# A routed two-layer network on one core: first quad of each pass taken through by itself, z moved between engines, dummy products added

## The reference, cut to what matters

```python
x = x + gnn(layernorm(x), adj, ...)   # matmul by e_weight, adjacency, then h = tanh(agg @ Wx + h @ Wh + b) over 128 steps
x = x + ffn(layernorm(x), ...)        # 16 experts, the best 2 of each token

# ffn, for its input z = layernorm(x):
topk_vals, topk_idx = top_k(z @ gate_w + gate_b, 2); topk_w = softmax(topk_vals)
h = relu(z @ w1[e] + b1[e]);  expert_out = h @ w2[e] + b2[e]
y = z + sum over the two experts of topk_w * expert_out
ffn = (y - mean(y)) / sqrt(var(y) + 1e-5) * gamma + beta
```

## Time and profile before

| | us |
|---|---|
| median of 3 runs (654.96 to 655.76) | 655.46 |
| the profiled execution | 655.11 |
| its span, first to last instruction | 653.4 |

### The profile page before, as it was taken

How to read it: one execution, slowest core, us unless ns; L and a number is a source line. 1 busy time by engine, 2 the same in 40 slices (tenths; PEclk the granted TensorE clock), 3 DMA queues, 4 the chain that set the end, 5 groups by cost and what they waited for, 6 DMA issues and landing times. The chain is left out here.

```text
span 653.4 us, 17215 instructions
## 1 busy us (share of the span) xinstructions
PE 535.4 (82%) x4144; PEld 476.4 (73%) x4144; DVE 507.6 (78%) x2512; ACT 411.0 (63%) x1343; POOL 451.3 (69%) x521
## 2 busy tenths in 40 slices
PE   1676799999889861799999999943899999999990
PEld 0566567776666650599999999941799999988890
DVE  4899269999999997488888888620499899898861
ACT  1898765555555533366666666710589889899860
POOL 8766307777777777277777777776177777777775
PEclk9988899889999965899999999975799999999995
DMA  8999913665355214479886665442997666764110
GB/s 208 254 285 271 287 50 102 213 200 170 118 168 114 88 54 124 111 241 346 264 257 198 208 199 188 153 157 72 338 332 246 216 200 204 220 187 140 48 54 15
DMA packets 112893, 119.26 MB, mean 183 GB/s; under 512 B 18346, under 2 KB 97406, under 8 KB 112801
## 3 DMA queue, kind: packets, MB, share of 16 engines
q1 hardware_dynamic: 93056, 73.55, 40.6%
q0 software_dynamic: 17152, 43.03, 18.1%
q10 hardware_dynamic: 2592, 1.64, 0.8%
HBM read 66.51 MB, written 53.77 MB: 184 GB/s over the span
## 5 line engine op out<-in xcount | busy, mean ns | idle before, releaser
L311 POOL DMA_INDIRECT out_dram<-R x136 | 135.0, 993 | 59.4 <-issue 52.2
L311 POOL DMA_INDIRECT rows_by_second<-R x136 | 136.2, 1001 | 54.2 <-issue 33.2
L311 POOL DMA_INDIRECT rows_by_first<-st x128 | 125.9, 984 | 64.4 <-issue 35.6
L1143 PE MATMUL bank<-xT,wr 128*128 128x128 f32 (+1 forms) x1152 | 155.6, 280 | 8.9 <-ACT xT L1218 8.9
L1163 PE MATMUL bank<-W,hs 128*128 x1024 | 156.9, 290 | 0.0
L1143 PEld LDWEIGHTS bank<-xT,wr 128*128 128x128 f32 x1152 | 140.8, 194 | 16.0 <-ACT xT L1218 16.0
L1243 ACT ACTIVATE hs<-bank,wr 128x128 f32<-128x128 f32 x380 | 111.8, 366 | 64.4 <-PE bank L1143 59.3
L1163 PEld LDWEIGHTS bank<-W,hs 128*128 128x128 f32 x1024 | 135.1, 192 | 3.1
L1228 ACT COPY wr<-W1b 128x258 f32 x288 | 103.5, 424 | 0.0
L1328 DVE SCALAR_TENSOR_TENSOR R<-bank,R 128x128 f32<-128x128 f32 x272 | 82.2, 344 | 24.5 <-PE bank L1163 24.5
L670 ACT ACTIVATE HT<-bank,bcol 128x128 f32<-128x128 f32 x128 | 47.0, 367 | 66.6 <-PE bank L573 65.6
(11 more groups left out here) (171 smaller groups left out, 896.2 us busy)
## 6 DMA issues: line engine op xcount, KB each, us to landing
R<-rows_by_second SPq DMA_DIRECT2D x122, 196.0 KB
R<-rows_by_first SPq DMA_DIRECT2D x124, 68.0 KB
xq<-in_x_dram SPq DMA_DIRECT2D x32, 256.0 KB, 4.1
aq<-in_adj_dram SPq DMA_DIRECT2D x32, 256.0 KB, 5.0
x2r<-in_x_dram SPq DMA_DIRECT2D x32, 256.0 KB, 2.9
rows_by_second<-filler SPq DMA_DIRECT2D x2, 1568.0 KB, 7.4
rows_by_second<-filler SPq DMA_DIRECT2D x16, 196.0 KB
rows_by_second<-R POOLq DMA_INDIRECT x136
```

The source lines that it names most:

```text
L311: return nc.gpsimd.indirect_dma_start(dst, bass.IndirectOffsetOnAxis(ap=idx, axis=0), src, None, bounds_check=limit[n], oob_is_err=False)
L1143: i = mm(ps_h[c][h][:, at:at + n], wr[:, u % 2, s, j, c * P:(c + 1) * P], xT[:, u % 2, j * P + lo:j * P + lo + n], start=True, stop=True)
```

## The change

1. The spare word becomes `C_SHIFT` = -mean * rstd. A new small VectorE operation, `shift`, writes it once per pair of turns at the end of `even`, in the scan.
2. z of the first pass moves to ScalarE: `zed` is now an activation with scale rstd and bias `C_SHIFT`. In return relu of the first pass is VectorE's alone (c = 0 and 1: 4 operations per half, 8 on half blocks).
3. The first quad of each pass is finished in its own turn: `second` of half 1 follows that of half 0 before the next quad is turned; `share`, and in the second pass `norm_a`, `root` and `norm_b`, of both halves stand in that turn too. From the third quad on the order is as before.
4. `awake` issues three dummy products behind the landing in the second pass, where it was one.

```diff
+            def shift(p):
+
+                dve.wait_ge(s_r2, p + 1)
+                v.scalar_tensor_tensor(out=two(p, C_SHIFT), in0=two(p, C_MEAN), scalar=-1.0, in1=two(p, C_RSTD),
+                                       op0=ALU.mult, op1=ALU.mult)
...
                 pair(ou_1, p)
+                pair(shift, p)
...
-                warm(1 if r else 2)
+                warm(3 if r else 2)
...
-                if q > 0:
+                if q > 1:
                     second(r, G - 1, 1, held[r] + e[0:2])
                 first(G, u, 1)
                 if q == 0:
                     second(r, G, 0, e[2:4])
+                    second(r, G, 1, experts(r, at + QUAD)[0:2])
...
+            def zed(G, u):
+
+                act.wait_ge(e_ld[u], loads_of(G))
+                for j in range(QUAD):
+                    i = a(R[:, u, j, C_Z:W_B], R[:, u, j, 0:P], ACT.Identity,
+                          scale=R[:, u, j, C_RSTD:C_RSTD + 1], bias=R[:, u, j, C_SHIFT:C_SHIFT + 1])
+                i.then_inc(e_z, 1)
...
+            def quad_0(q, G, u, last):
+                if q == 0:
+                    begin_pass(0, q, G, u)
+                if last:
+                    return
+                e = experts(0, q + 1)
+                v = (u + 1) % RING
+                zed(G + 1, v)
+                weights(0, q + 1, G + 1, v, 0, e)
+                weights(0, q + 1, G + 1, v, 1, e)
+                turn_out(G + 1, v)
+                weights(0, q + 1, G + 1, v, 2, e)
+                weights(0, q + 1, G + 1, v, 3, e)
...
+            def quad_0(q, G, u, last):
+                before = (u - 1) % RING
+                if q == NPURE:
+                    dve.wait_ge(e_mix, 2)
+                if q == 0:
+                    add_beta(G, u)
+                relu(G, u, 0)
+                if q > 1:
+                    share(0, G - 1, before, 1)
+                relu(G, u, 1)
+                if q > 0:
+                    add_beta(G, u)
+                share(0, G, u, 0)
+                if q == 0 or last:
+                    share(0, G, u, 1)
```

More of the change, by code:

```diff
@@ L22 @@
 LN_EPS = 1e-5
[L25 removed]
+C_MEAN, C_RSTD, C_W1, C_W2, C_TOKEN, C_POS1, C_POS2, C_SHIFT = range(P, P + 8)
 W_A = P + 8
@@ L1257, in experts, with begin_pass @@
                 return e + numbers(act, et_act[0:1, r, at + QUAD:at + 2 * QUAD]) if mixed(q) else e
-            def quad(r, q, G, u, last):
-                start = isinstance(q, int) and q == 0
-                if start:
[L1262 to L1267, removed]
+            def begin_pass(r, q, G, u):
+                e = experts(r, q)
+                for j in range(QUAD):
+                    weights(r, q, G, u, j, e)
+                loads(r)
+                if r == 0:
+                    zed(G, u)
+                turn_out(G, u)
@@ L1268, in quad, with quad_1 @@
+            def quad_1(q, G, u, last):
+                start = q == 0
+                if start:
+                    begin_pass(1, q, G, u)
+                if q == NPURE:
                     act.wait_ge(e_mix, 2)
-                e = None if last else experts(r, q + 1)
+                e = None if last else experts(1, q + 1)
                 v = (u + 1) % RING
-                relu(r, G, u, 0)
-                if r == 1 and not start:
+                relu(G, u, 0)
+                if start:
+                    relu(G, u, 1)
+                elif q > 1:
@@ L1273, in quad @@
                     root(G - 1, 0)
+                if not last:
+                    weights(1, q + 1, G + 1, v, 0, e)
+                    weights(1, q + 1, G + 1, v, 1, e)
                 if start:
[L1275 to L1280, removed]
+                    root(G, 0)
+                else:
+                    relu(G, u, 1)
@@ L1281, in quad @@
                 if not last:
                     turn_out(G + 1, v)
-                    weights(r, q + 1, G + 1, v, 2, e)
-                    weights(r, q + 1, G + 1, v, 3, e)
-                if r == 1 and not start:
+                    weights(1, q + 1, G + 1, v, 2, e)
+                    weights(1, q + 1, G + 1, v, 3, e)
+                if q > 1:
                     root(G - 1, 1)
-                if last and r == 1:
+                if start:
+                    root(G, 1)
+                if last:
@@ L1288, in quad @@
                     root(G, 0)
                     root(G, 1)
+            def quad(r, q, G, u, last):
+                if r:
+                    quad_1(q, G, u, last)
+                else:
+                    quad_0(q, G, u, last)
             passes(act, quad)
@@ new lines, in quad_1 @@
+            def quad_1(q, G, u, last):
+                before = (u - 1) % RING
+                if q == 0:
+                    relu(G, u, 0)
+                    relu(G, u, 1)
+                if q > 1:
+                    share(1, G - 1, before, 1)
+                    norm_b(G - 1, before, 0)
+                    norm_a(G - 1, before, 1)
+                share(1, G, u, 0)
+                norm_a(G, u, 0)
+                if q > 1:
+                    norm_b(G - 1, before, 1)
+                if q == 0:
+                    norm_b(G, u, 0)
+                    share(1, G, u, 1)
+                    norm_a(G, u, 1)
+                    norm_b(G, u, 1)
+                if last:
+                    share(1, G, u, 1)
+                    norm_b(G, u, 0)
+                    norm_a(G, u, 1)
+                    norm_b(G, u, 1)
```

66 lines of the change are left out of this document (18 added, 48 removed).

## The result

| | before | changed |
|---|---|---|
| median of 12 runs, us | 655.13 (653.92 to 658.24) | 659.39 (656.21 to 661.94) |
| ratio, 95% interval | | 1.0062 (1.0042 to 1.0082) |
| profiled execution, us | 655.11 | 656.21 |

The change costs 4.1 us (2.8 to 5.4). The profiled execution happens to be the shortest of the changed kernel's twelve, so its sum must not be taken for the result. It also entered the scan early: its first `place_3` starts at 96.56 us, where it was 97.82. Stages are therefore compared by distances.

A forecast was written before the change was run, and what follows sets the result against it. GpSimd's conveyor of 136 scatters was taken to bound each pass, so only its start counts; VectorE hardly waits in the scan. +2.8 + 0.45 - 0.75 = +2.5 on 655.11, plus 0.35 for the median: 658.0 us, range 656.0 to 660.6.

The forecast's parts named there:

- The shift: Scan on VectorE: 14 of 16 shift operations cost 0.20 us each, delaying tables and bias parts by 2.8 us (1.5 to 3.2).
- The turn: First pass: all five dummies stand behind the bias parts, so the turn moves from 269.74 to about 272.5, +2.8 us.
- third rival: Slower by more: the clock rises late and dummies hold the turn in both passes; +4.95 us, 660.4 us, chance 0.15.
- z and the dummies meet within 0.1 us: Before the first pass's turn at 269.74, five dummies and the first four z operations end at about the same time.
- z on ScalarE: First pass: four z cost 1.28 us against 1.1 on VectorE, end about 271, ahead of the turn at 272.5; cost nothing.
- the 1.2 us that I gave: What z's later end on ScalarE would cost at the first pass's turn without the late dummies.
- The first pass's first quads: Relu on VectorE alone, first quad finished first: second quad's rows reach the conveyor late, +0.45 us (-0.26 to +1.5).
- The second pass: Three dummies and the new order: first scatter 4.4 us earlier, but the second quad limits the gain to -0.75 us (0 to -1.4).
- The rule: VectorE's two-port mode locks GpSimd from writing descriptors; moving z could gain far more than the rows' 1.1 us; sum took zero.
- The first two rivals: No change that can be told, 655.9 us, chance 0.19; and faster, 653.5 us, chance 0.08.
- A shift hidden by pipelining: In the scan each shift operation costs only 0.11 us, 1.5 us in all; sum +0.45, 655.9 us, chance 0.19.
- The early first quad carried through to the end: Second pass: conveyor starts at 467.1 instead of 471.53 and keeps most of 4.4 + 0.8 us; 653.5 us, chance 0.08.

The follow-up runs named there:

- moved wait: TensorE waits for the bias parts behind the dummies: on the changed kernel ratio 1.0001, 655.47 against 655.81 for the kernel before; on the kernel before ratio 1.0016, +1.0 us.
- the swap alone: Changed kernel with the old first-quad order and one dummy, leaving the shift, z on ScalarE and relu on VectorE: ratio 1.0036, +2.4 us against the kernel before.

## Why the prediction was right, and where it was off

Time (658.0 forecast, 659.39 measured), side and range were right. The mechanism that decides, the shift through the bias parts to the dummies and the turn, was right too. That the sum came so near is in part luck: forecast was +2.5 us, measured +4.1 and +3.2; the shift cost less than forecast (+2.0 for +2.8), and the second pass cost where a gain of 0.75 us stood in the sum.

**The shift.** Forecast +2.8 us on the chain of tables and bias parts. At the last `place_3` it was 2.69 and 2.73 us against the trace of before, by the spacing named; at the end of the bias parts 2.4 us against that trace, and 2.0 us between the means of the traces with and without the shift. It was the term that carries the result, and over-sized by some 0.8 us against the runs: from the last `place_3` to the bias parts it takes 13.9 us with the shift and 14.3 in six of the nine traces without, and three of these nine had the long scan, of those with the shift none. Why is not shown.

**The turn.** I moved the whole block of dummies by 2.8 us and kept its length of 6.2 us. The traces show 7.31 and 6.49 us for the changed kernel. It looks like the half of my third rival that is about the first pass, but it is not the change's doing: the clock's rise is not at a fixed distance from the first dummy in any of the kernels. That z and the dummies meet within 0.1 us was a reading of one execution; it is so in two of the six traces with neither shift nor moved wait, and in the other four the dummies hold the turn for 0.8 to 1.5 us behind the end of z. With the shift z is 3.0 to 4.2 us ahead of the turn in all four traces whose dummies wait for the bias parts. Measured from the first `place_3`, the turn stands at 172.5 us without and at 174.9 us with the shift (means of these six and four): +2.4 us, where I had +2.8. That the wait for the bias parts carries this is shown by the moved wait, which is worth 3 to 4 us in the changed kernel and nothing (-1 us) in the kernel before.

**z on ScalarE.** I priced four at 1.28 us, from a copy with a scale; with scale and bias they took 1.64 us. It hung on nothing. My estimate of 271 us for its end was 3 us late: the loads were issued from 263.5 on, between the copies of the weights, where before all four stood behind them (265.4). Without late dummies it would not have cost the 1.2 us that I gave either: with the wait moved z ended 171.5 us behind the first `place_3`, as it does on VectorE in the nine traces without the shift (171.5 to 171.9).

**The first pass's first quads.** Forecast +0.45 us at the fifth scatter, measured +0.63 and +0.67 us (12.81 and 12.85 for 12.18). The experiments split it: the new order with relu on both engines gives 0 (12.18), relu on one engine with the old order +0.3 (12.50).

**The second pass.** Here a step failed: "**-0.75 us**, out of 4.4 us won at the first scatter". The trace agrees to the tenth (first scatter 8.76 us behind the turn, forecast 8.7; seventh 21.06, forecast 21.1), though the wait before the fifth was 3.8 us and not 2 to 3. But I had taken the gain of a full clock and the effect of the new order as one thing, against a single execution of the kernel before at half clock. In the second pass of the seven traces with one dummy the clock fell within 0.2 us of the turn in two, 1.0 to 1.5 us behind it in three, and not at all in two; at full clock the old order stands at 20.25. In all five traces with the change's three dummies it was at full at the turn and for at least 7 us behind it: that part of the forecast held. So the new order loses 0.8 us where I had it winning: relu of the second quad comes 7.9 us behind the turn in the old order (469.50 - 461.57) and 9.6 us in the new one (470.33 - 460.75), behind the square root that I had named but set against the half-clock row of 9.6. Over the runs the order of the second pass costs 1.6 us, and the dummies bring 1.0 us that is not clear of zero.

**The rest.** The shift (+2.0), the swap (+0.4), the new order (+2.2) and the dummies (-1.0) make +3.6 us, between the two measurements of the change, +4.1 and +3.2. Each of the four is uncertain by about 1 us, and they come from three chips, so this agreement is no proof of the parts.

**The rule.** By the Trainium skill, page "SBUF — State Buffer", section "SBUF: two separate sides", z taken off VectorE could have freed GpSimd's descriptor writing by much more than the 8 ns per scatter of the rows. The four traces with z on ScalarE have 996 to 1003 ns per scatter of the first pass, the ten with z on VectorE 1000 to 1013 ns. That is 8 ns at the means, 1.1 us in the pass, as the bound from the rows had it, where my sum had zero. It is not the rule's doing: in the trace of before 56 of the 136 scatters of the first pass run beside a z operation, and they average 987 ns, the 80 others 1011 ns. No lockout by whole operations shows.

**The first two rivals.** A shift hidden by pipelining did not happen. The early first quad carried through to the end did not either: the four scatters went out early and the conveyor then stood for 3.8 + 1.3 us.

## What to carry to other kernels

On an engine that is nowhere idle, price a small operation by what hangs on the end of its list, not by its length: here 16 of 0.17 us moved the bias parts, the dummies and a turn by 2.0 to 2.4 us in the mean. A conveyor fed by a pipeline gains nothing from an early first item if the second comes no earlier. When a clock state is part of the comparison, take the base in the same state before crediting an edit with the difference; a second trace of the same kernel shows which rows are the edit's and which the execution's.

## What was new of the hardware

From the first dummy product of the first pass, with TensorE busy from there on, to the granted clock's rise to full it took from 3.0 us (the shift alone: 266.16, full at 269.2) to 6.2 us (the swap alone: 266.68, full at 272.9) in executions of nearly the same program. From the first of the five dummies to the turn it took 5.9 to 7.4 us accordingly. The clock also fell in stretches that were mostly busy: at 473.8 after waits of 1.26 and 0.54 us, and at 467.8 in the kernel with three dummies after waits of 0.92 and 0.68 us.

Where the 4 to 6 us of spread between executions of one kernel arise can be read in part from the fourteen traces. The first `place_3` starts at 96.1 to 98.9 us. The clock first rises at 20.8 to 22.0 us in seven of them, whose first `place_3` is at 96.9 us in the mean, and at 26.0 to 27.5 us in the other seven, where it is at 98.0. A half clock from 175 to 182 us goes with 1.4 us more of scan, late dummies with up to 1.5 us at the first turn. So a good part of the spread goes with the clock; that the clock is its cause was not tested.
